# Graph layer with layernorm: the first two tiles on unsplit x in plain fp32, and the order of the first loads

## The chip, the cores and the metric

The kernel runs on one core of one Trainium2 chip. The metric is the time of one execution on the device in microseconds (us). The kernel before took 436.32 us, the median of three runs (435.46 to 437.48).

## The reference

Inputs are x (4096 x 256) and adj (4096 x 4096), both fp32. adj is nonnegative and mostly zero.

```python
def _L0_gnn_ref(cur, incidence_m):
    mask = incidence_m > 0
    head = mask.astype(incidence_m.dtype)
    head = head / jnp.maximum(jnp.sqrt(jnp.sum(head * head, axis=-1, keepdims=True)), EPS)
    inc = incidence_m + head
    edge_fea = inc @ cur
    edge_degree = jnp.sum(inc, axis=-1, keepdims=True)
    return edge_fea / edge_degree
x = _layernorm(x + _L0_gnn_ref(x, adj), axis=-1)
```

So each row of adj gets 1/sqrt(count of its positive entries) added at those entries, is multiplied with x, divided by its sum, added to x's row, and normalised.

## The kernel before, in words

**Tiling.** The output has 32 tiles of 128 rows. A tile of adj is held as `raw[:, s, k, :]`: a slot s (two, by the tile's parity) and four quarters k of 32 rows each. On the partitions a quarter is spread by columns: partition group g (32 partitions) holds columns 1024 g to 1024 g + 1023. A quarter is loaded by four DMAs of 128 KB, one for each g, in the order 0, 2, 1, 3 (L151 to L152). A 32 x 32 block transpose of the quarters gives `incT`, and its 32 blocks b are the weights of 32 steps of accumulation over the 4096 columns.

**A tile's steps.** ScalarE takes the sign of each quarter and sums it by partition (L209). TensorE sums over partition groups with `quad_sum` (`sum_signs` L533 at the start, `sum_quadrants` L545 later; the latter also sums the rows of `inc`). VectorE makes the count (L400), GpSimd takes the power 0.5 (L311), called norm. ScalarE multiplies the quarter by the norm into PSUM (L218, two buffers `scaled`). VectorE forms `inc` in units of the norm, (raw > 0) + scaled, with its row sum (L412), and transposes it (L422). The norm's factor falls out in the division by the sum.

**Products.** Of the 32 blocks six are multiplied in plain fp32 with `x_native` (L558, two instructions each, in the array `edge[s]`, columns 0 to 255). The other 26 (SPLIT) go as three products of rounded values (fp32r): incT is split in `inc_hi` (rounded, ScalarE L225 for quarters 0 and 3, GpSimd L335 for 1 and 2) and `inc_lo` (the rest, GpSimd L330), and x in high and low parts in `x_split`. One product of `inc_hi` with both parts of x (L584, 512 columns) and one of `inc_lo` with x's high part (L587, 256 columns) make one block. VectorE then adds up the residual: degree (L435), reciprocal (L439), two steps that read `edge` (L445, L449), statistics, and after GpSimd's power -0.5 (L315) the result (L470).

**Start.** SP's queue issues the four quarters of tile 0, then x's blocks 0 to 15 into slot 1 of incT, the six native blocks, tile 1, x's blocks 16 to 25 into `rows`, tile 2, and behind a wait for x's low part the residual rows. x's split is done in three chunks by ScalarE (L255), GpSimd (L341, L343, L369) and VectorE (L385). Tile 0's count and norm are taken of all four quarters at once. Tiles 0 and 1 then go as all others do, except that VectorE makes tile 0's low quarters 2 and 3 (L394).

**What sets the order.** The order of each engine's work is written out by hand; engines are tied by semaphores alone. On TensorE the sums of tile t stand behind the fourth native block of tile t, and wait for the signs of tile t + 2 (L540). VectorE's count of tile t + 1 stands behind its third `inc` quarter of tile t. GpSimd's norm of tile t + 1 is the first thing in its tile t. From tile 2 the engines run loops over pairs of tiles.

## Time and profile before

| | us |
|---|---|
| Median of three runs | 436.32 |
| The profiled execution | 437.03 |
| Its span, first to last instruction | 435.2 |
| TensorE busy | 392.1 |
| VectorE busy | 368.6 |
| GpSimd busy | 369.4 |
| ScalarE busy | 347.8 |

The mean granted clock of TensorE was 0.98 of full speed. In the profile PE is TensorE's matmul, DVE VectorE, ACT ScalarE, POOL GpSimd, SP SyncE; SPq is SP's queue of DMA issues. Busy time is a sum over the span; where it isn't spread evenly the timeline has to be read beside it. A row of a timeline has start, duration, engine, line, what is written and read, and in brackets how long the engine was idle before it and what released it.

### The profile page before, as it was taken

Reading aid. Unit: us, or ns where it says so; the run is one execution under the profiler, and the core shown is the slowest. Engines: PE = TensorE matmul, PEld = TensorE weight load, DVE = VectorE, ACT = ScalarE, POOL = GpSimd, SP = SyncE. Lnnn points to the kernel's source line nnn. Section 1 sums busy time; section 2 is a strip of 40 time slices with the busy share of each in tenths; the row PEclk is TensorE's granted clock in tenths of the full one; section 3 lists DMA queues with packets and bytes.
Section 4 is the critical chain, followed back from the end, with each engine's and each line's share of the span. In section 5 each row is a group of like instructions: output and inputs, shape, how many; then the busy total and the mean of one; then the engine's idle time right before and its main releaser. Section 6 shows DMA issues by size and latency. Waiting matters only on the chain.

```text
span 435.2 us, 8833 instructions
## 1 busy us (share of the span) xinstructions
PE 392.1 (90%) x2148; PEld 343.6 (79%) x2148; DVE 368.6 (85%) x739; ACT 347.8 (80%) x452; POOL 369.4 (85%) x274
## 2 busy tenths in 40 slices
PE   0056479999999999999999999999999999999995
PEld 0036368888888888888888888888888888888884
DVE  0436788999999999999999999999999999999932
ACT  4655899889888998988998888898889988886200
POOL 1096878999999999999999999999999999999860
PEclk9996789999999999999999999999999999999999
DMA  7999575566667766666666666666666666670010
GB/s 198 218 265 256 172 221 184 174 197 191 191 208 207 217 195 196 192 193 194 195 194 193 199 202 217 206 185 207 189 194 193 192 195 196 199 213 24 24 39 12
DMA packets 38090, 79.84 MB, mean 183 GB/s; under 512 B 9408, under 2 KB 21696, under 8 KB 38080
## 3 DMA queue, kind: packets, MB, share of 16 engines
q1 hardware_dynamic: 38080, 79.73, 63.0%
q14 instruction: 7, 0.06, 0.1%
q8 instruction: 3, 0.05, 0.0%
HBM read 75.50 MB, written 4.19 MB: 183 GB/s over the span
## 4 chain that ended last, share of the span: by engine, by line
PE 84%; SPq 5%; issue 5%; DMA 3%; DVE 2%; ACT 0%; POOLq 0%; POOL 0%; ACTq 0%; DVEq 0%
PE edge L584 42%; PE edge L587 22%; PE edge L558 19%; DMA rows<-in_x_dram 3%; SPq L152 3%; SPq L171 1%; PE sums L545 1%; DVE inc L412 1%; DVE incT L422 1%; SPq L168 1%; SPq L175 0%; ACT scaled L218 0%; POOLq L46 0%; POOL rstd L315 0%; DVE rows L449 0%
## 5 line engine op out<-in xcount | busy, mean ns | idle before, releaser
L584 PE MATMUL edge<-x_split,inc_hi 128*128 128x512 f32 (+1 forms) x864 | 304.4, 399 | 4.1 <-POOL x_split L369 2.7
L330 POOL TENSOR_TENSOR inc_lo<-incT,inc_hi 128x832 fp32r<-128x832 f32 x126 | 248.7, 1985 | 12.1 <-DVE incT L422 7.7
L587 PE MATMUL edge<-x_split,inc_lo 128*128 128x256 f32 x832 | 235.8, 283 | 0.0
L584 PEld LDWEIGHTS edge<-x_split,inc_hi 128*128 128x128 f32 x864 | 165.0, 191 | 40.6 <-POOL x_split L369 3.0
L209 ACT ACTIVATE sign_out<-raw,sign_bias 128x1024 bf16<-128x1024 f32 x128 | 146.4, 1144 | 35.4 <-DMA raw<-in_adj_dram 33.9
L412 DVE SCALAR_TENSOR_TENSOR inc<-raw,scaled 128x1024 f32<-128x1024 f32 x128 | 153.6, 1202 | 9.3 <-ACT scaled L218 9.3
L587 PEld LDWEIGHTS edge<-x_split,inc_lo 128*128 128x128 f32 x832 | 160.1, 192 | 0.0
L422 DVE STREAM_TRANSPOSE incT<-inc 128x1024 f32<-128x1024 f32 x128 | 155.4, 1227 | 0.0
L218 ACT ACTIVATE scaled<-raw,norm 128x1024 f32<-128x1024 f32 x128 | 141.6, 1108 | 9.7 <-DVE inc L412 5.3
L558 PE MATMUL edge<-x_native,incT 128*128 128x256 f32 x384 | 97.5, 394 | 11.9 <-DMA x_native<-in_x_dram 11.9
L558 PEld LDWEIGHTS edge<-x_native,incT 128*128 128x128 f32 x384 | 69.9, 194 | 20.7 <-DVE incT L422 12.0
L225 ACT CAST inc_hi<-incT 128x832 fp32r<-128x832 f32 x64 | 56.5, 884 | 13.0 <-DVE incT L422 9.0
L311 POOL TENSOR_TENSOR norm<-count,half 128x4 f32<-128x4 f32 x32 | 34.6, 1080 | 28.5 <-DVE count L400 28.5
L335 POOL TENSOR_SCALAR inc_hi<-incT 128x832 fp32r<-128x832 f32 x64 | 58.7, 918 | 0.0
L445 DVE SCALAR_TENSOR_TENSOR rows<-edge,rdeg,rows 128x256 f32<-128x256 f32 x32 | 15.5, 483 | 31.4 <-PE edge L587 31.4
L315 POOL TENSOR_TENSOR rstd<-var_eps,minus_half 128x1 f32<-128x1 f32 x32 | 18.0, 562 | 11.8 <-DVE var_eps L461 11.8
L209 ACT ACTIVATION_READ_ACCUMULATOR sign_out<-raw,sign_bias 128x1 f32 x128 | 23.9, 187 | 0.0
L470 DVE TENSOR_SCALAR rows<-rows,mean_var,rstd 128x256 f32<-128x256 f32 x32 | 20.9, 654 | 1.3 <-POOL rstd L315 1.3
L545 PEld LDWEIGHTS sums<-part_sums,quad_sum 128*128 128x128 f32 x64 | 12.2, 194 | 7.5 <-DVE incT L422 3.3
L400 DVE TENSOR_SCALAR count<-sums 128x4 f32<-128x4 f32 x32 | 4.9, 153 | 15.3 <-PE sums L533 14.0
L533 PE MATMUL sums<-part_sums,quad_sum 128*128 128x4 f32 x4 | 0.9, 307 | 16.6 <-ACT sign_out L209 16.6
L449 DVE SCALAR_TENSOR_TENSOR rows<-edge,rdeg,rows 128x256 f32<-128x256 f32 x32 | 15.4, 480 | 0.1
(30 smaller groups left out, 86.6 us busy)
## 6 DMA issues: line engine op xcount, KB each, us to landing
raw<-in_adj_dram SPq DMA_DIRECT2D x512, 128.0 KB, 2.6
rows<-in_x_dram SPq DMA_DIRECT2D x32, 128.0 KB, 2.1
out_dram<-rows SPq DMA_DIRECT2D x32, 128.0 KB, 1.8
incT<-in_x_dram SPq DMA_DIRECT2D x4, 512.0 KB, 9.9
rows<-in_x_dram SPq DMA_DIRECT2D x4, 320.0 KB, 12.3
x_native<-in_x_dram SPq DMA_DIRECT2D x4, 192.0 KB, 10.8
```

The costliest lines, as they stand in the source:

```text
L209: nc.scalar.activation(sign_out[:, :], raw[:, s, q, :], ACT.Sign, scale=SIGN_SCALE, bias=sign_bias[:, 0:1], accum_out=part_sums[:, s, 1, q ...
L218: nc.scalar.mul(scaled[q % 2][:, :], raw[:, s, q, :], norm[:, s, q:q + 1]).then_inc(scaled_ready, 1)
L225: nc.scalar.copy(hi_of(s, q), incT[:, s, 0:SPLIT, q, :]).then_inc(hi_by_act, 1)
L311: nc.gpsimd.tensor_tensor(norm[:, s, :], count[:, s, :], half[:, :], ALU.pow).then_inc(norm_ready, 1)
L330: nc.gpsimd.tensor_tensor(inc_lo[:, s, :, q, :], incT[:, s, 0:SPLIT, q, :], hi_of(s, q).bitcast(fp32), ALU.subtract).then_inc(lo_by_pool, ...
L335: nc.gpsimd.tensor_scalar(hi_of(s, q), incT[:, s, 0:SPLIT, q, :], 1.0, 1.0, ALU.mult, ALU.mult).then_inc(hi_by_pool, 1)
L412: nc.vector.scalar_tensor_tensor(inc[:, q, :], raw[:, s, q, :], 0.0, scaled[q % 2][:, :], ALU.is_gt, ALU.add, accum_out=part_sums[:, s, 0, ...
L422: nc.vector.transpose(incT[:, s, :, q, :], inc[:, q, :].rearrange("p (b j) -> p b j", j=SQ)).then_inc(incT_ready, 1)
L470: nc.vector.tensor_scalar(result[:, s, :], y[:, s, :], mean_var[:, s, 0:1], rstd[:, s:s + 1], ALU.subtract, ALU.mult).then_inc(result_read ...
L558: last = nc.tensor.matmul(edge[s][:, 0:D], incT[:, s, SPLIT + n, :, :].rearrange("p q j -> p (q j)"), x_native[:, n, :], start=(n == 0), s ...
L584: nc.tensor.matmul(edge[s][:, c0:c1], inc_hi[:, s, b, :, :].rearrange("p q j -> p (q j)"), x_split[:, b, :, :].rearrange("p h d -> p (h d) ...
L587: last = nc.tensor.matmul(edge[s][:, D:2 * D], inc_lo[:, s, b, :, :].rearrange("p q j -> p (q j)"), x_split[:, b, 0, :], start=False, stop ...
```

## The change

Tiles 0 and 1 multiply all 32 blocks in plain fp32 with unsplit x (`native_tile`). x's 26 other blocks land in a buffer `x_stage` of their own (it shares its place with the second slot of the split adjacency, which is first written for tile 3) in four chunks of 7, 7, 6 and 6 blocks, and TensorE takes them chunk by chunk. x is split later, behind the scales of tile 1: high parts by ScalarE, low parts by GpSimd (chunks 0, 1) and VectorE (2, 3). Tile 0's count and norm are made quarter by quarter. Tile 0's loads are issued half by SP and half by ScalarE. SP's order is tile 0, native x, tile 1, the chunks of x (partition groups in the order 0, 2, 1, 3), the residual rows of tiles 0 and 1, tiles 2 and 3. Rounding of adjacency begins with tile 2, and the sums of tiles 0 and 1 are placed at blocks 12 and 26 of tile 1. The residual of tiles 0 and 1 has one step in place of two, as there are no second columns of `edge`. The loops of ScalarE, GpSimd and TensorE begin at tile 4; tiles 2 and 3 are written out. The rest of the diff (counters moved by one, names) follows from this.

```diff
--- before.py
+++ after.py
...
         x_split = sb("x_split", [P, SPLIT, 2, D], fp32r)
         x_native = sb("x_native", [P, NATIVE, D], fp32)
-
-        rows = sb("rows", [P, max(7, SPLIT - B // 2), D], fp32)
+        inc_split0 = sb("inc_split0", [P, 2, SPLIT, G, SQ], fp32r)
+
+        with nc.sbuf_tensor("x_stage", [P, SPLIT, D], fp32) as x_stage:
+            pass
+        inc_split1 = sb("inc_split1", [P, 2, SPLIT, G, SQ], fp32r)
+        inc_split = [inc_split0, inc_split1]
+
+        rows = sb("rows", [P, 7, D], fp32)
...
+        X_AT = [0, 7, 14, 20, SPLIT]
+        X_LO_POOL = [0, 1]
+        X_LO_DVE = [2, 3]
 
...
 
+        def x_staged(c):
+            return x_stage[:, X_AT[c]:X_AT[c + 1], :]
+
         def hi_of(s, q):
-            return inc_hi[:, s, :, q, :]
+            return inc_split[s][:, 0, :, q, :]
+
...
-
             for k in range(G):
-                load_quarter(0, 0, k, False)
-            for g in range(G):
-                sp.dma_start(incT[SQ * g:SQ * (g + 1), 1, :, :, :].rearrange("p b q j -> p (b q j)"),
-                             x_v[g, :, 0:X_AT[2], :]).then_inc(x_in[0], 16)
-            for g in range(G):
+                for g in (0, 1):
+                    load_piece(sp, 0, 0, k, g)
+            for g in PORT_ORDER:
                 sp.dma_start(x_native[SQ * g:SQ * (g + 1), :, :], x_v[g, :, SPLIT:B, :]).then_inc(x_native_in, 16)
             for k in range(G):
                 load_quarter(1, 1, k, False)
-            for g in range(G):
-                sp.dma_start(rows[SQ * g:SQ * (g + 1), 0:SPLIT - X_AT[2], :],
-                             x_v[g, :, X_AT[2]:SPLIT, :]).then_inc(x_in[1], 16)
+            for c in range(4):
+                for g in PORT_ORDER:
+                    sp.dma_start(x_stage[SQ * g:SQ * (g + 1), X_AT[c]:X_AT[c + 1], :],
+                                 x_v[g, :, X_AT[c]:X_AT[c + 1], :]).then_inc(x_in[c], 16)
+            for s in range(2):
+                load_residual(s, s, False)
             for s in range(2):
                 for k in range(G):
                     load_quarter(2 + s, s, k, True)
-
-                sp.wait_ge(x_lo_by_pool, 2)
-                load_residual(s, s, False)
...
+            for k in range(G):
+                for g in (2, 3):
+                    load_piece(act, 0, 0, k, g)
+            act.wait_ge(consts_ready, 1)
+
+            nc.scalar.activation(table_load[:, :], sign_bias[:, :], ACT.Sign)
+
+            sign_quarter(0, 0, 0, 0, first=True, reuse=False)
+            sign_quarter(0, 0, 0, 1, reuse=False)
+            scale_quarter(0, 0, 0, first=True)
+            sign_quarter(0, 0, 0, 2, reuse=False)
+            scale_quarter(0, 0, 1, first=True)
+            sign_quarter(0, 0, 0, 3, reuse=False)
+            scale_quarter(0, 0, 2, first=True)
+            scale_quarter(0, 0, 3, first=True)
             for q in range(G):
-                sign_quarter(0, 0, 0, q, first=(q == 0), reuse=False)
-
-            def split_x_hi(c):
-
-                act.wait_ge(x_in[c // 2], X_CHUNK)
...
-            scale_quarter(0, 0, 0, False)
-            scale_quarter(0, 0, 1, False)
-            scale_quarter(0, 0, 2, False)
-            scale_quarter(0, 0, 3, False)
-            round_quarter(0, 0, 0, False)
-            split_x_hi(1)
-            for q in range(3):
                 sign_quarter(1, 1, 0, q, reuse=False)
-            round_quarter(0, 0, 3, False)
-            sign_quarter(1, 1, 0, 3, reuse=False)
-            split_x_hi(2)
-
-            scale_quarter(1, 1, 0, True)
-            scale_quarter(1, 1, 1, True)
-            sign_quarter(2, 0, 1, 0)
-            scale_quarter(1, 1, 2, True)
-            scale_quarter(1, 1, 3, True)
-            sign_quarter(2, 0, 1, 1)
-            round_quarter(1, 1, 0, False)
-            sign_quarter(2, 0, 1, 2)
-            sign_quarter(2, 0, 1, 3)
-            round_quarter(1, 1, 3, False)
-            scale_quarter(2, 0, 0, True)
-            scale_quarter(2, 0, 1, True)
+            for q in range(G):
+                scale_quarter(1, 1, q)
+            for c in range(4):
+                split_x_hi(c)
+
+            for q in range(G):
+                sign_quarter(2, 0, 1, q, reuse=False)
+            scale_quarter(2, 0, 0)
+            scale_quarter(2, 0, 1)
             sign_quarter(3, 1, 1, 0)
             sign_quarter(3, 1, 1, 1)
...
+            tile(2, 0, 1, reuse=False)
+            tile(3, 1, 1, staged=True)
+            with act.Fori(2, PAIRS - 1) as u:
...
+            for q in range(G):
+                pool.wait_ge(first_count, q + 1)
+                nc.gpsimd.tensor_tensor(norm[:, 0, q:q + 1], count[:, 0, q:q + 1], half[:, 0:1],
+                                        ALU.pow).then_inc(first_norm, 1)
             norm_of(1, 1)
-
-            pool.wait_ge(x_hi_by_act, 2)
-            nc.gpsimd.tensor_tensor(x_part(2, 1), x_stage(2), x_part(2, 0).bitcast(fp32),
-                                    ALU.subtract).then_inc(x_lo_by_pool, 1)
-            tile(1, 1, reuse=False)
-            with pool.Fori(1, PAIRS - 1) as u:
+            for c in X_LO_POOL:
+                split_x_lo(c)
+            norm_of(2, 0)
+            tile(2, 0, reuse=False)
+            tile(3, 1, staged=True)
+            with pool.Fori(2, PAIRS - 1) as u:
...
-                yield
-                after(3)
-                nc.vector.scalar_tensor_tensor(y[:, s, :], edge[s][:, 0:D], rdeg[:, :], y_main[:, :],
-                                               ALU.mult, ALU.add).then_inc(y_ready, 1)
+                if native:
+                    nc.vector.scalar_tensor_tensor(y[:, s, :], edge[s][:, 0:D], rdeg[:, :], xres[:, s, :],
...
+            first_count_of(0)
+            first_count_of(1)
+            inc_quarter(0, 0, 0, False, False)
+            first_count_of(2)
+            transpose_quarter(0, 0, 0, False, False)
+            inc_quarter(0, 0, 1, False, False)
+            first_count_of(3)
+            transpose_quarter(0, 0, 1, False, False)
+            inc_quarter(0, 0, 2, False, False)
+            transpose_quarter(0, 0, 2, False, False)
+            inc_quarter(0, 0, 3, False, False)
+            transpose_quarter(0, 0, 3, False, False)
+            count_of(1, 1)
+            for q in range(G):
+                inc_quarter(1, 1, q, True, False)
+                transpose_quarter(1, 1, q, False, False)
+            for c in X_LO_DVE:
+                split_x_lo(c)
+            count_of(2, 0)
+            tile(2, 0, 1, native=True, slot_split=False, norm_before=False)
+            tile(3, 1, 1, native=True, slot_split=False, reuse_result=False)
...
+            def native_tile(t, s, middle):
 
                 pe.wait_ge(incT_ready, G * t + G)
-                if reuse:
-
-                    pe.wait_ge(y_ready, t - 1)
+                if t == 0:
+                    pe.wait_ge(x_native_in, FOUR_DMAS)
+                for n in range(NATIVE):
+                    if n in middle:
+                        middle[n]()
+                    native_matmul(s, SPLIT + n, x_native[:, n, :], n == 0, False)
+                for b in range(SPLIT):
+                    if t == 0 and b in X_AT:
+                        pe.wait_ge(x_in[X_AT.index(b)], FOUR_DMAS)
+                    if NATIVE + b in middle:
+                        middle[NATIVE + b]()
+                    last = native_matmul(s, b, x_stage[:, b, :], False, b == SPLIT - 1)
+                return last
...
+            def split_products(t, s, first):
+
+                pe.wait_ge(lo_by_pool, G * (t - FIRST_SPLIT) + G)
...
+
+                    pe.wait_ge(x_lo_by_pool, len(X_LO_POOL))
+                    pe.wait_ge(x_lo_by_dve, len(X_LO_DVE))
...
+            for q in range(G):
+                sum_first(q)
+            native_tile(0, 0, {3: lambda: sum_signs(1, 1)}).then_inc(edge_ready, 1)
+            native_tile(1, 1, {12: lambda: sum_quadrants(0, 0, reuse=False, first=True),
+                               26: lambda: sum_quadrants(1, 1, reuse=False)}).then_inc(edge_ready, 1)
+            tile(2, 0, first=True)
+            tile(3, 1)
+            with pe.Fori(2, PAIRS - 1) as u:
```

## Rows read from the trace of the kernel before

**Rows 1.** Page, part 1: busy time of TensorE.

```profile
PE 392.1 (90%) x2148; PEld 343.6 (79%) x2148; DVE 368.6 (85%) x739; ACT 347.8 (80%) x452; POOL 369.4 (85%) x274
```

**Rows 2.** Waits of TensorE: line, releaser, us in total, times, longest.

```profile
PE edge L558 <- DMA x_native<-in_x_dram: 11.9, 1, 11.9
...
PE edge L584 <- POOL x_split L369: 2.7, 1, 2.7
```

**Rows 3.** Timeline of TensorE: start, us, line, idle before it.

```profile
25.95 5.46 PE L558 MATMUL edge<-x_native,incT 128*128 128x256 f32 x12 [11.94 <-DMA x_native<-in_x_dram]
...
37.11 0.63 PE L584 MATMUL edge<-x_split,inc_hi 128*128 128x512 f32 x1
...
37.75 0.63 PE L584 MATMUL edge<-x_split,inc_hi 128*128 128x512 f32 x1
...
51.33 0.56 PE L545 MATMUL sums<-part_sums,quad_sum 128*128 128x8 f32 x2 [3.00 <-DVE incT L422]
...
61.43 0.36 PE L545 MATMUL sums<-part_sums,quad_sum 128*128 128x8 f32 x2 [2.30 <-issue]
...
72.32 1.89 PE L558 MATMUL edge<-x_native,incT 128*128 128x256 f32 x8
74.05 0.28 PE L545 MATMUL sums<-part_sums,quad_sum 128*128 128x8 f32 x2
...
74.95 0.59 PE L584 MATMUL edge<-x_split,inc_hi 128*128 128x256 f32 x2
...
429.70 0.28 PE L587 MATMUL edge<-x_split,inc_lo 128*128 128x256 f32 x1
```

**Rows 4.** Busy by window: PE, PEld, DVE, ACT, POOL, granted clock, DMA share, GB/s.

```profile
62.50:65.80 3.30, 3.30 (x12) 2.82 (x12) 3.30 (x8) 3.30 (x5) 3.08 (x3) 0.50 0.47 140
96.20:418.20 322.00, 322.00 (x1811) 283.85 (x1811) 301.70 (x616) 277.01 (x361) 301.00 (x217) 1.00 0.61 185
```

**Rows 5.** Timeline of ScalarE: first steps that waited for a load.

```profile
4.88 1.15 ACT L209 ACTIVATE sign_out<-raw,sign_bias 128x1024 bf16<-128x1024 f32 x1 [1.12 <-DMA raw<-in_adj_dram]
...
12.06 1.15 ACT L209 ACTIVATE sign_out<-raw,sign_bias 128x1024 bf16<-128x1024 f32 x1 [1.13 <-DMA raw<-in_adj_dram]
...
27.66 1.15 ACT L209 ACTIVATE sign_out<-raw,sign_bias 128x1024 bf16<-128x1024 f32 x1 [3.43 <-DMA raw<-in_adj_dram]
...
39.22 2.32 ACT L255 CAST x_split<-rows 128x2560 fp32r<-128x2560 f32 x1 [4.75 <-DMA rows<-in_x_dram]
...
53.23 2.16 ACT L218 ACTIVATE scaled<-raw,norm 128x1024 f32<-128x1024 f32 x2 [0.43 <-POOL norm L311]
```

**Rows 6.** The same windows view, three stretches of the first loads.

```profile
14.00:16.00 2.00, 0.01 (x1) 0.00 (x0) 0.16 (x1) 0.64 (x1) 1.04 (x1) 1.00 1.12 216
26.00:28.00 2.00, 2.00 (x5) 1.65 (x6) 0.00 (x0) 0.34 (x1) 2.00 (x1) 1.00 1.06 289
44.00:46.00 2.00, 0.69 (x4) 0.33 (x3) 2.00 (x3) 2.00 (x4) 2.00 (x1) 1.00 0.30 88
```

**Rows 7.** Timeline of SyncE: the issue of tile 0's loads.

```profile
0.73 7.36 SPq L152 DMA_DIRECT2D raw<-in_adj_dram  x16
```

**Rows 8.** Timeline of VectorE: first and last of tile 0's eight operations.

```profile
16.51 1.22 DVE L412 SCALAR_TENSOR_TENSOR inc<-raw,scaled 128x1024 f32<-128x1024 f32 x1 [2.31 <-ACT scaled L218]
...
23.36 2.37 DVE L422 STREAM_TRANSPOSE incT<-inc 128x1024 f32<-128x1024 f32 x2
```

**Rows 9.** Timeline of GpSimd: norm of tile 2, then its first and last low quarters.

```profile
52.18 1.02 POOL L311 TENSOR_TENSOR norm<-count,half 128x4 f32<-128x4 f32 x1 [0.47 <-DVE count L400]
...
63.30 1.98 POOL L330 TENSOR_TENSOR inc_lo<-incT,inc_hi 128x832 fp32r<-128x832 f32 x1 [0.22 <-DVE incT L422]
...
69.63 3.93 POOL L330 TENSOR_TENSOR inc_lo<-incT,inc_hi 128x832 fp32r<-128x832 f32 x2
```

**Rows 10.** Page, part 5: line, operation, count, busy, mean ns of one.

```profile
L225 ACT CAST inc_hi<-incT 128x832 fp32r<-128x832 f32 x64 | 56.5, 884 | 13.0 <-DVE incT L422 9.0
...
L209 ACT ACTIVATION_READ_ACCUMULATOR sign_out<-raw,sign_bias 128x1 f32 x128 | 23.9, 187 | 0.0
```

More of the change, by code:

```diff
@@ L430, in after @@
                 def after(k):
[L432 to L434 removed]
+                    dve.wait_ge(dve_step, steps_to(t) + k - (1 if native and k > 2 else 0))
+                dve.wait_ge(summed, t + 2)
                 step(nc.vector.scalar_tensor_tensor(deg_pick[:, :], sums[s][:, 0:G], 1.0, own_quarter[:, :],
```

269 lines of the change are left out of this document (122 added, 147 removed).

## The prediction

> **What bounds the kernel now.** I read the page first: TensorE is busy 90% of a 435.2 us span [rows 1]. An average doesn't say where the other tenth is, so next came the list of waits of TensorE. All its larger waits lie in the first 62 us: 11.9 us for the native part of x and 2.7 us for the low part of x's third chunk [rows 2]; the timeline adds 3.0 us for the transposes of tile 1 and 2.3 us ahead of that tile's sums, and shows the rest: tile 0 starts at 25.95, tile 2 at 72.32, and the last product starts at 429.70, about 430.0 with its tail [rows 3]. So the 30 tiles 2 to 31 take 357.7 us, 11.92 each, and no wait stands among them. From 72.32 on TensorE sets the pace; before that the start does. The change can gain only what it takes off the start of tile 2, and what it adds before that costs nothing as long as tile 2 is ready earlier.
>
> Two prices come out of the same rows. Four native blocks go from 72.32 to 74.05, 0.433 us each. A whole tile less its six natives (2.60) and its sums (0.14) leaves 9.18 us for 26 split blocks, 0.353 each. Those are at the full clock (2.4 GHz). At the half clock the twelve native instructions from 25.95 take 5.46 us, 0.88 to 0.91 a block [rows 3], and one split block 0.64 us (37.11 to 37.75) [rows 3]. The granted clock was 0.50 in 62.5 to 65.8 too, right behind the gap that ended at 61.43 [rows 3, 4]: a gap of two to three microseconds in TensorE's work is followed by some 3 us at half clock. For those 3.3 us TensorE does work worth 1.8 us.
>
> **The terms.** (1) *Plain products for tiles 0 and 1.* Each has 32 blocks of 0.433, 13.9 us, in place of 11.8: 2.1 us more per tile, 4.2 in all at full clock. In exchange tile 0 needs no rounding, no low parts and no split x. Those were what spread tile 0 of before over 25.95 to about 56.4. TensorE is the cover of nothing here; it is fed by the loads.
>
> (2) *Order of loads.* Before, ScalarE's signs show the landings: tile 0's quarters at 4.9 to 12.06, the first quarter of tile 1 at 27.66, the last chunk of x at 39.22 [rows 5]; tile 2's data were in about 44.6 (the last window moves 0.18 MB, 0.6 us at full rate) [rows 6]. Rows of x (1 KB each) came at 216 GB/s, adjacency at 289 [rows 6]. Now tile 1 comes ahead of the 2.10 MB of x that stood before it: 9.7 us at 216 GB/s earlier, so its last quarter lands about 23 and not 33, and its signs end about 24.2. The last chunk of x has the same bytes ahead of it as before. Tile 2 has 0.26 MB more ahead, the two residual tiles, which SP now issues first and without their wait for x's low part: 1.2 us.
>
> (3) *Two queues for tile 0.* SP issued 16 loads in 7.36 us, 0.46 each [rows 7]; the halving of the first four saves 0.9 us at the front. The first four quarters land 2.4 us apart (7.2 us for three) [rows 5], more than the 1.84 that SP needs to issue four, so behind the first quarter it is the transfers that count. I take 0.5 us for all the stream, bounds 0 and 1.1. The eight issues sit on ScalarE ahead of the table load, and can move its first sign from 4.88 to about 6; tile 0's norm by quarters gains more than that (its scale no longer waits for the fourth sign), and TensorE has slack there, next. The Trainium skill (DMA: Bandwidth & Descriptors, section Issuing engines are not separate DMA queues) says that issuing from several engines saves only the time of issuing. By that rule the term would be 0.9 us at most; by a doubled rate of the first 2.1 MB it would be over 4.
>
> (4) *Tile 0.* VectorE's eight operations take 9.2 us in a chain (16.51 to 25.73 before) [rows 8]. Started some 6 us sooner they end about 19 to 20.5. TensorE then does three native blocks and waits in the middle of tile 0 for the signs of tile 1 (24.2). So the start of tile 0 is hidden, and neither the norm by quarters nor the second queue can move the end: their worth in the sum is nil. If tile 1's loads weren't there the cover would be gone, and VectorE's 20 would count.
>
> (5) *TensorE up to the sums of tile 0.* These now stand at block 12 of tile 1. From 24.4 it has 29 blocks of tile 0 and 12 of tile 1. With 5.3 us at half clock (6 blocks) and 35 at 0.433, 20.5 us: 44.9, if x is never late. By the last chunk of x (39.2 less 0.5, then 6 + 12 blocks, 7.8 us) it is 46.5. The same sums wait for tile 2's four signs: data at 44.6 + 1.2 − 0.5 = 45.3, the last sign 1.15 us: 46.4. Three roads meet at about 46.5, which I take (bounds 44.9 and 49).
>
> (6) *From there a new chain.* Sums to norm 0.85 and 1.05 for the norm (51.33, 52.18, 53.23): scale of tile 2 starts at 48.4 [rows 3, 5, 9]. ScalarE then has two scales (2.16), two signs, a scale, two signs; a sign takes 1.15 and 0.19 for its accumulator read when another sign follows, a scale 1.1 [rows 5, 10]. That is 8.3 us: 56.7. The sums of tile 1 (block 26) wait for exactly these four signs of tile 3; TensorE is there at 46.5 + 0.3 + 14 x 0.433 = 52.9, a **new wait of 3.8 us**. Queued behind that wait are the last six blocks of tile 1. VectorE waits for the same sums in its count of tile 3, with the transposes of quarters 1 to 3 of tile 2 behind it, and GpSimd waits for that count in its norm of tile 3, with all rounding of tile 2 behind it. Norm 57.6 to 58.6; then GpSimd's low and rounded quarters of tile 2, which took 63.30 to 73.56 before (last row 69.63 + 3.93), 10.3 us [rows 9]: **ready at 69.0 and not 73.56**. TensorE's natives of tile 2 start at about 62.8 (transposes) and hold the sums that wait for tile 4's signs: one round of ScalarE (four signs, four scales of 1.1, two roundings of 0.88: 10.9 us) behind 56.7, 67.6; then sums and two native blocks at half clock: **split blocks from 69.8, not 74.95** [rows 3]. Gain 5.1.
>
> (7) *The clock.* TensorE idles before 56.7, before 62.8 and before 67.6, so by the rows of (1) the split blocks start at half clock. I take 1.8 us lost (bounds 0 and 2.4).
>
> (8) *Behind tile 2.* TensorE ends tile 2 at 69.8 + 9.2 + 1.8 = 80.8 against 84.24 before. Then it needs tile 3's low parts at 83.5: GpSimd's next round of 11.3 us ends at 80.3. In the steady part GpSimd is busy 301 of 322 us [rows 4], 11.1 of each 11.92, so it can follow a TensorE that is ahead but can't catch up if it is late itself. Nothing else in the loops changes.
>
> **Sum.** 84.24 − 80.8 = 3.4 us earlier. The profiled execution took 437.03, 1.83 more than its span and 0.71 over the median 436.32. 437.03 − 3.4 = 433.6; against the median 432.9. That is the forecast: of a start that looks 15 us better for tile 0, some 3 arrive. Its own range is 431 to 435.
>
> **Rivals.**
> *A, slower: the half clock in tile 1's plain products.* x's chunks (0.92 MB each, 4.2 us at 216 GB/s) come slower than TensorE eats them at full clock (7 x 0.433 = 3.0 us), so it idles over 1 us per chunk. For: the natives at 25.95 stayed at half speed for all of their 5.4 us, and short idle stretches were followed by clock 0.50 [rows 3, 4]. Against: at half clock seven blocks take 6.2 us, longer than a chunk, so TensorE has no gap then and warms again. If the last 6 and the first 12 blocks run at half clock, the sums of tile 0 come 18 x 0.45 = 8 us later, and all of (6) with them: 432.9 + 8 = 440.9. It decides from 3.4 us of loss on, eight cold blocks.
>
> *B, faster: x lands sooner and the clock holds.* Before, x was loaded in the order of partitions 0, 32, 64, 96, 512 KB at a time, at 216 GB/s; the adjacency, in the order 0, 64, 32, 96, at 289 [rows 6]. The change gives x that second order as well. If it is the order and not the packet's size that makes the rate, x's 4.19 MB come 4.9 us sooner, TensorE is never starved in tile 0, and (5) gives 44.9, 1.6 us more; with a warm clock in (7) another 1.8: 432.9 − 3.4 = 429.5. The Trainium skill (SBUF — State Buffer, section Door 1: The DMA port swizzle) has partitions 32 apart on the same ports and 64 apart on others; by that rule this rival's first half happens. The start of the stream, in the better order and at 0.52 MB per 2.4 us, 219 GB/s [rows 5], speaks against counting on all of it.
>
> *C, no change: the new chain is longer than I have it.* It has some 20 links from tile 2's last sign to tile 2's low part, on four engines. GpSimd was busy 301 of 322 us in the steady part [rows 4], so nothing lost there comes back. Three microseconds more (late landings of tiles 2 and 3, tile 2's products cold throughout) give 436. That the first tiles gain nothing at all, because the last x chunk lands as late as before, is the same case.
>
> **How the numbers follow.** Forecast 0.45, A 0.13, B 0.22, C 0.20. Measurement can tell about 0.5% (2.2 us) of this kernel from no change, so faster is below 434.1: the forecast but for its upper end, and B: 0.62. Same: C and the upper end of the forecast, 0.25. Slower: A, 0.13. The range takes B with its bounds and leaves out most of A: 428.5 to 438.
>
> **What would show it.** The step on loads: ScalarE's first sign of tile 1 near 17 to 18, last chunk of x near 38.7 (B: near 34). Step 5: sums of tile 0 near 46.5 (A: over 52). Step 6: a wait of 3 to 4 us of TensorE for a sign of tile 3, GpSimd's last low part of tile 2 ending near 69. Step 7: granted clock 0.50 somewhere in 57 to 73. Step 8: tile 3 starting near 80.8, tiles of 11.92 behind it with no wait. If a wait appears in those, or if the sums of tile 0 come after 50, the prediction is wrong.

## The result and the profile after

The changed kernel takes 432.73 us against 436.83 (medians of 20 runs each): ratio 0.9903, 95% interval [0.9889, 0.9917], 4.1 us faster. Its profiled execution took 431.71, 1.0 under its median, where the one of before lay within 0.7 of its own; so the 5.3 us between the two spans (435.2 and 429.9) are more than the change brings as a rule.

TensorE, start, duration, line, idle before it; these rows answer to [rows 3]:

```profile
20.55 2.93 PE L577 MATMUL edge<-x_native,incT 128*128 128x256 f32 x6 [6.43 <-DVE incT L436]
...
29.24 6.15 PE L577 MATMUL edge<-x_stage,incT 128*128 128x256 f32 x26 [0.54 <-DMA x_stage<-in_x_dram]
36.15 2.86 PE L577 MATMUL edge<-x_stage,incT 128*128 128x256 f32 x12 [0.76 <-DMA x_stage<-in_x_dram]
38.84 2.75 PE L577 MATMUL edge<-x_native,incT 128*128 128x256 f32 x12
...
46.34 0.36 PE L572 MATMUL sums<-part_sums,quad_sum 128*128 128x8 f32 x2 [2.16 <-issue]
...
56.29 0.36 PE L572 MATMUL sums<-part_sums,quad_sum 128*128 128x8 f32 x2 [1.75 <-issue]
...
61.71 1.99 PE L577 MATMUL edge<-x_native,incT 128*128 128x256 f32 x8 [0.85 <-DVE incT L436]
66.75 0.36 PE L572 MATMUL sums<-part_sums,quad_sum 128*128 128x8 f32 x2 [3.04 <-DVE incT L436]
...
68.23 0.79 PE L618 MATMUL edge<-x_split,inc_split 128*128 128x256 f32 x2
...
78.75 1.89 PE L577 MATMUL edge<-x_native,incT 128*128 128x256 f32 x8
```

Tile 0 is done at 38.84, where before it was at about 56.4. Tile 3 starts at 78.75 against 84.24: of 17.6 us at the end of tile 0 a third is left two tiles later. The rows between show where it goes: TensorE stands at the sums of tile 0 (46.34), at those of tile 1 (56.29), for the transposes of tile 2 (61.71) and at the sums of tile 2 (66.75). The profile puts the first of them down to "issue" and the last to VectorE's transposes; the first names no engine and the last one whose work had long been done; the semaphore that came last was that of ScalarE's signs, as the next rows show.

ScalarE; these rows answer to [rows 5]:

```profile
17.78 1.15 ACT L220 ACTIVATE sign_out<-raw,sign_bias 128x1024 bf16<-128x1024 f32 x1 [0.36 <-DMA raw<-in_adj_dram]
...
36.12 1.48 ACT L247 CAST x_split<-x_stage 128x1536 fp32r<-128x1536 f32 x1 [0.55 <-DMA x_stage<-in_x_dram]
39.09 1.15 ACT L220 ACTIVATE sign_out<-raw,sign_bias 128x1024 bf16<-128x1024 f32 x1 [1.49 <-DMA raw<-in_adj_dram]
...
45.01 1.15 ACT L220 ACTIVATE sign_out<-raw,sign_bias 128x1024 bf16<-128x1024 f32 x1 [0.96 <-DMA raw<-in_adj_dram]
...
54.95 1.15 ACT L220 ACTIVATE sign_out<-raw,sign_bias 128x1024 bf16<-128x1024 f32 x1
...
65.41 1.15 ACT L220 ACTIVATE sign_out<-raw,sign_bias 128x1024 bf16<-128x1024 f32 x1
```

The last sign of tile 2 waits for its load until 45.01 and ends at 46.16; the sums of tile 0 start at 46.34. The last sign of tile 3 (54.95) ends at 56.10, the sums of tile 1 start at 56.29; the last of tile 4 ends at 66.56, the sums of tile 2 start at 66.75. Three times TensorE starts 0.2 us behind a sign.

GpSimd; these rows answer to [rows 9]:

```profile
56.93 1.01 POOL L324 TENSOR_TENSOR norm<-count,half 128x4 f32<-128x4 f32 x1 [8.93 <-DVE count L408]
58.08 1.96 POOL L344 TENSOR_TENSOR inc_split<-incT,inc_split 128x832 fp32r<-128x832 f32 x1
...
64.32 3.86 POOL L344 TENSOR_TENSOR inc_split<-incT,inc_split 128x832 fp32r<-128x832 f32 x2
```

GpSimd idles 8.93 us for the count of tile 3, then needs 10.1 us and has the low parts of tile 2 at 68.18; TensorE's split blocks start at 68.23. By window (busy time of PE, PEld, DVE, ACT, POOL, then granted clock, DMA share, GB/s; compare [rows 4, 6]):

```profile
2.00:12.00 10.00, 1.73 (x6) 1.50 (x6) 1.57 (x5) 6.73 (x10) 2.18 (x9) 1.00 1.04 278
28.00:34.00 6.00, 5.46 (x25) 4.17 (x24) 5.93 (x8) 4.72 (x4) 1.30 (x1) 1.00 1.13 240
46.00:56.00 10.00, 8.19 (x30) 6.60 (x30) 5.77 (x13) 8.03 (x12) 1.01 (x1) 0.83 0.81 226
58.00:62.00 4.00, 3.15 (x8) 1.98 (x8) 4.00 (x8) 4.00 (x6) 3.92 (x4) 0.62 0.37 107
66.00:71.00 5.00, 4.15 (x16) 3.38 (x17) 5.00 (x12) 4.59 (x7) 4.99 (x4) 0.69 0.81 250
96.20:418.20 322.00, 322.00 (x1812) 283.01 (x1811) 299.28 (x614) 271.74 (x354) 298.54 (x215) 1.00 0.59 181
```

The first 10 us of loads run at 278 GB/s and x in 28 to 34 at 240, against 216 for x before [rows 6]; the clock falls three times behind TensorE's waits (0.83, 0.62, 0.69 as means of these windows), and the steady part is what it was: TensorE busy 322.00 of 322 us.

### The profile page after: what moved, and what is told of

Read it like the earlier page. It is cut to its first block, busy times and chain, and to the rows that moved or that the text cites. A ratio compares the mean times of both kernels' runs of the same rounds, so it can differ in the third digit from the quotient of the medians.

```text
span 429.9 us, 8836 instructions
## 1 busy us (share of the span) xinstructions
PE 396.9 (92%) x2152; PEld 344.8 (80%) x2152; DVE 371.7 (86%) x739; ACT 346.5 (81%) x450; POOL 351.1 (82%) x266
## 3 DMA queue, kind: packets, MB, share of 16 engines
q10 hardware_dynamic: 384, 1.05, 0.8%
## 4 chain that ended last, share of the span: by engine, by line
PE 84%; SPq 5%; issue 4%; POOL 2%; DMA 2%; DVE 1%; POOLq 0%
PE edge L618 41%; PE edge L577 21%; PE edge L621 21%; SPq L187 3%; SPq L157 2%; DMA x_stage<-in_x_dram 2%; POOL inc_split L344 2%; PE sums L572 1%; SPq L182 0%; POOL inc_split L349 0%; DVE incT L436 0%; POOL rstd L328 0%; POOLq L45 0%; DVE rows L463 0%; DVE rows L467 0%
## 5 line engine op out<-in xcount | busy, mean ns | idle before, releaser
L618 PE MATMUL edge<-x_split,inc_split 128*128 128x512 f32 (+1 forms) x810 | 281.4, 396 | 0.1
L344 POOL TENSOR_TENSOR inc_split<-incT,inc_split 128x832 fp32r<-128x832 f32 x120 | 237.2, 1987 | 10.5 <-DVE incT L436 7.6
L621 PE MATMUL edge<-x_split,inc_split 128*128 128x256 f32 x780 | 218.3, 280 | 0.0
L618 PEld LDWEIGHTS edge<-x_split,inc_split 128*128 128x128 f32 x810 | 152.9, 189 | 34.9 <-POOL inc_split L344 0.6
L220 ACT ACTIVATE sign_out<-raw,sign_bias 128x1024 bf16<-128x1024 f32 x128 | 146.4, 1144 | 32.4 <-DMA raw<-in_adj_dram 30.9
L621 PEld LDWEIGHTS edge<-x_split,inc_split 128*128 128x128 f32 x780 | 147.7, 189 | 0.0
L242 ACT CAST inc_split<-incT 128x832 fp32r<-128x832 f32 x60 | 53.2, 886 | 11.8 <-DVE incT L436 7.3
L349 POOL TENSOR_SCALAR inc_split<-incT 128x832 fp32r<-128x832 f32 x60 | 55.2, 920 | 0.0
L463 DVE SCALAR_TENSOR_TENSOR rows<-edge,rdeg,rows 128x256 f32<-128x256 f32 x30 | 14.5, 484 | 31.0 <-PE edge L621 31.0
L577 PE MATMUL edge<-x_stage,incT 128*128 128x256 f32 x104 | 27.4, 422 | 1.6 <-DMA x_stage<-in_x_dram 1.6
L577 PEld LDWEIGHTS edge<-x_stage,incT 128*128 128x128 f32 x104 | 21.3, 209 | 6.5 <-DMA x_stage<-in_x_dram 3.2
L488 DVE TENSOR_SCALAR rows<-rows,mean_var,rstd 128x256 f32<-128x256 f32 x32 | 21.8, 681 | 1.3 <-POOL rstd L328 1.3
L355 POOL TENSOR_TENSOR x_split<-x_stage,x_split 128x1792 fp32r<-128x1792 f32 x2 | 9.5, 4772 | 7.7 <-ACT x_split L247 7.7
```

Of the source, the lines that this page charges most:

```text
L220: nc.scalar.activation(sign_out[:, :], raw[:, s, q, :], ACT.Sign, scale=SIGN_SCALE, bias=sign_bias[:, 0:1], accum_out=part_sums[:, s, 1, q ...
L242: nc.scalar.copy(hi_of(s, q), incT[:, s, 0:SPLIT, q, :]).then_inc(hi_by_act, 1)
L344: nc.gpsimd.tensor_tensor(lo_of(s, q), incT[:, s, 0:SPLIT, q, :], hi_of(s, q).bitcast(fp32), ALU.subtract).then_inc(lo_by_pool, 1)
L349: nc.gpsimd.tensor_scalar(hi_of(s, q), incT[:, s, 0:SPLIT, q, :], 1.0, 1.0, ALU.mult, ALU.mult).then_inc(hi_by_pool, 1)
L488: nc.vector.tensor_scalar(result[:, s, :], y[:, s, :], mean_var[:, s, 0:1], rstd[:, s:s + 1], ALU.subtract, ALU.mult).then_inc(result_read ...
L577: return nc.tensor.matmul(edge[s][:, 0:D], incT[:, s, b, :, :].rearrange("p q j -> p (q j)"), x_of_b, start=start, stop=stop)
```

## The experiments

The times are medians, those of the kernel before beside them 436.25 to 436.83; "changed" is the changed kernel. From the timelines of each profile come the marks: the start of the last sign of tile 2 on ScalarE, of the sums of tiles 0 and 1 and of tile 3 on TensorE, and the end of the low parts of tile 2 on GpSimd. The chain is low parts less sums of tile 0; the last column but one is from there to tile 3's start.

| kernel | last sign of tile 2 | sums, tile 0 | sums, tile 1 | low parts, tile 2 | tile 3 | chain | then | us |
|---|---|---|---|---|---|---|---|---|
| changed | 45.01 | 46.34 | 56.29 | 68.18 | 78.75 | 21.8 | 10.6 | 432.73 |
| after_again | 45.96 | 47.30 | 57.24 | 69.35 | 78.69 | 22.1 | 9.3 | 433.10 |
| one_queue | 45.39 | 46.73 | 56.88 | 68.77 | 80.73 | 22.0 | 12.0 | 433.23 |
| x_order | 48.83 | 50.17 | 60.32 | 72.22 | 83.90 | 22.1 | 11.7 | 433.63 |
| norm_at_once | 43.46 | 44.80 | 55.16 | 67.26 | 78.01 | 22.5 | 10.8 | 431.14 |
| resid_late | 44.94 | 46.28 | 56.22 | 68.13 | 78.51 | 21.9 | 10.4 | 431.15 |
| more_plain | 41.74 | 45.98 | 55.85 | 67.95 | 77.13 | 22.0 | 9.2 | 432.69 |
| more_plain20 | 46.34 | 53.15 | 63.01 | 74.91 | 85.66 | 21.8 | 10.8 | 438.04 |
| reorder | 46.59 | 47.93 | 59.26 | 68.26 | 83.14 | 20.3 | 14.9 | 436.05 |
| best1 | 43.15 | 44.49 | 56.20 | 65.49 | 80.46 | 21.0 | 15.0 | 436.35 |
| reorder2 | 47.37 | 48.71 | 60.14 | 69.28 | 78.83 | 20.6 | 9.6 | 432.26 |
| best2 | 44.04 | 45.38 | 57.03 | 66.17 | 75.59 | 20.8 | 9.4 | 430.91 |
| best3 | 43.14 | 44.48 | 55.91 | 65.26 | 74.85 | 20.8 | 9.6 | 430.82 |

One difference ties the marks to the times. The time of the profiled execution less the start of tile 3 is 352.8 us in the kernel before (437.03 less 84.24) and 352.7 to 353.0 in the changed kernel and the seven below it, down to more_plain20: there the start of tile 3 carries the whole difference. In reorder and best1 it is 353.8 and 353.3, in reorder2, best2 and best3 354.8, 355.0 and 356.1: these three lose 2 to 3 us again behind the start of tile 3.

**The changed kernel once more** (no edit).

> The changed kernel as it is, beside the others of this set. Its profiles so far: from the sums of tile 0 to tile 2's last low part 21.8 to 22.5 us in five kernels, and from there to tile 3's start 10.4 to 12.0. Theory (a rigid chain): the same here, 21.8 to 22.5. Rival (the chain breathes with the loads): over 23 or under 21.

433.10 us, ratio 0.9912 [0.9884, 0.994]. The chain is 22.1, as expected. Over the eight kernels that leave it alone it is 21.8 to 22.5 while its start moves between 44.8 and 53.15: step 6's road is rigid. What follows it is not (9.2 to 12.0), though it is the same 26 blocks.

**One queue for tile 0.**

```diff
             for k in range(G):
-                for g in (0, 1):
-                    load_piece(sp, 0, 0, k, g)
+                load_quarter(0, 0, k, False)
...
-            for k in range(G):
-                for g in (2, 3):
-                    load_piece(act, 0, 0, k, g)
```

> The changed kernel with all 16 loads of tile 0 issued by SyncE and none by ScalarE. My theory now: the start is tied to the stream of loads (tile 2's last sign waits for a load at 45.01 in the changed kernel), and two queues moved 0.40 MB more by 12 us than one queue did before, 1.4 us of stream. So everything from the x chunks on lands 0.9 to 1.4 us later, the sums of tile 0 go from 46.3 to about 47.4, and the kernel takes 1.1 us more. Rival 1: two queues save only the time of issuing: at most 0.9 us. Rival 2: the front of the stream is hidden: 0.

433.23, ratio 0.9923 [0.9897, 0.995]. By window (columns as above), its loads ran at 250 GB/s in 2 to 12 us:

```profile
2.00:12.00 10.00, 1.73 (x6) 1.50 (x6) 1.95 (x6) 6.02 (x11) 2.35 (x10) 1.00 0.91 250
```

With two queues it was 278, and 265 to 283 in all twelve profiles with two queues: 0.28 MB, 1.2 us at 240 GB/s. That is more than the 0.9 us of issuing that I had put down for the first quarter, but issuing isn't ruled out as the cause. One queue issues 128 KB per 0.46 us [rows 7], 285 GB/s at most, over all of tile 0, and the DMA share was 0.91 where it was 0.99 to 1.05 with two; no run separates the pace of issuing from the rate of transfer. In time little can be seen: x's last chunk started to be rounded at 36.30 (changed: 36.12), tile 2's last sign at 45.39 (45.01), both less than the profiles differ among themselves, and the 0.5 us by the medians lies inside both intervals. The rate is shown; that it brings anything in time is not.

**Order of x's pieces.**

```diff
-            for g in PORT_ORDER:
+            for g in range(G):
                 sp.dma_start(x_native[...], ...)
...
-                for g in PORT_ORDER:
+                for g in range(G):
                     sp.dma_start(x_stage[...], ...)
```

> The changed kernel with the loads of x (chunks and native blocks) in the order of partition groups 0, 1, 2, 3 in place of 0, 2, 1, 3. If the order makes the rate, x's 4.19 MB fall back from 240 GB/s to the 216 of the kernel before: 1.9 us more of stream, last chunk of x landing near 38 and not 36.1, sums of tile 0 near 48.2, kernel 1.9 us slower. If the rate is that of 1 KB rows whatever their order: no change in rate (240) and time.

433.63, ratio 0.9937 [0.9912, 0.9962]: 0.9 us slower than the changed kernel by the medians, 1.5 by the ratios, with intervals that just overlap. Its profiled execution took 436.74, 3.1 over its median, so its marks (last chunk at 38.41, sums of tile 0 at 50.17) show the direction, not the size. Busy time, clock, DMA share and GB/s by window:

```profile
28.00:34.00 6.00, 6.00 (x27) 4.96 (x25) 5.89 (x9) 4.46 (x4) 0.55 (x1) 1.00 1.14 220
```

220 against 240 GB/s with nothing but the order different; the twelve profiles in the other order have 230 to 263 in this window, so 220 lies below them all. So both expectations are half right: the order makes about a tenth of the rate of x, and most of the distance to the 289 GB/s of the adjacency [rows 6] is left. That this rest is due to the 1 KB rows is likely, but no run changes their size alone. The Trainium skill's rule on ports (SBUF — State Buffer, Door 1: The DMA port swizzle) agrees in direction.

**Tile 0's norm at once.**

```diff
             sign_quarter(0, 0, 0, 1, reuse=False)
-            scale_quarter(0, 0, 0, first=True)
             sign_quarter(0, 0, 0, 2, reuse=False)
-            scale_quarter(0, 0, 1, first=True)
             sign_quarter(0, 0, 0, 3, reuse=False)
+            scale_quarter(0, 0, 0, first=True)
+            scale_quarter(0, 0, 1, first=True)
```

> The changed kernel with ScalarE's four signs of tile 0 ahead of its scales, so that the norm by quarters brings nothing. My theory (term 4): VectorE ends tile 0 some 2.3 us later (22.8, not 20.5), TensorE has 2.2 us of slack ahead of the sums of tile 0, so the time changes by 0 to 0.3 us. Rival: TensorE's start sets the end: 2.3 us slower.

431.14, ratio 0.9884 [0.9858, 0.9909]. By the timeline TensorE starts tile 0 at 22.44 and not 20.55, and doesn't wait for x behind it:

```profile
22.44 2.93 PE L577 MATMUL edge<-x_native,incT 128*128 128x256 f32 x6 [10.16 <-DVE incT L436]
25.16 0.43 PE L557 MATMUL sums<-part_sums,quad_sum 128*128 128x4 f32 x2
25.45 2.15 PE L577 MATMUL edge<-x_native,incT 128*128 128x256 f32 x6
27.43 11.39 PE L577 MATMUL edge<-x_stage,incT 128*128 128x256 f32 x52
38.66 2.75 PE L577 MATMUL edge<-x_native,incT 128*128 128x256 f32 x12
```

Tile 0 ends at 38.66, where the changed kernel ends it at 38.84: two microseconds of start are gone without a trace. The norm by quarters brings nothing here. That the kernel is 1.6 us faster by the medians, 0.8 by the ratios, isn't explained; the intervals overlap, and its profile had tile 2's last quarter 1.5 us sooner than the changed kernel's, which this edit doesn't touch.

**Residual rows behind tile 2.**

```diff
-            for s in range(2):
-                load_residual(s, s, False)
             for s in range(2):
                 for k in range(G):
                     load_quarter(2 + s, s, k, True)
+                if s == 0:
+                    for r in range(2):
+                        load_residual(r, r, False)
```

> The changed kernel with the two residual loads (0.26 MB) issued behind tile 2's loads in place of ahead of them. My theory: tile 2's last quarter gates the chain signs, sums of tile 0, norm, scales; it lands 1.1 us earlier, the sums of tile 0 go from 46.3 to 45.2 and the kernel gains 1.1 us. Rival: TensorE's own work or x's last chunk gates: no change.

431.15, ratio 0.9874 [0.9841, 0.9907]: 1.6 us under the changed kernel by the medians, with overlapping intervals. Its own profile doesn't show the gain (last sign of tile 2 at 44.94); the profiles of reorder and best1, and of reorder2 and best2, which differ by this edit alone, have it 3.4 and 3.3 us earlier. One profile each is thin: over all kernels whose loads aren't changed the mark lies between 41.74 and 47.37. In time reorder to best1 is nothing and reorder2 to best2 1.35 us.

**Ten and twenty more plain products.** They stand ahead of block 6 of tile 1 and write columns that nobody reads, so the output is unchanged.

```diff
+                    if t == 1 and b == 0:
+                        for n in range(10):
+                            nc.tensor.matmul(edge[s][:, D:2 * D], incT[:, s, n, :, :]...,
+                                             x_stage[:, n, :], start=False, stop=False)
```

> The changed kernel with ten more plain products (10 x 0.433 = 4.3 us at full clock) in tile 1, ahead of the sums of tile 0; they write columns of the array that nothing reads. My theory: TensorE has 0.8 to 2.2 us of slack there, so that the price of the plain products shows only beyond it: sums of tile 0 near 48.5 to 49, kernel 2.1 to 3.5 us slower. If TensorE's work in tiles 0 and 1 were not near the path at all: 0. If it were all on it: 4.3.

432.69, ratio 0.9903 [0.9879, 0.9928]: the ten cost nothing that can be measured (the intervals leave room for 1 us); I had expected 2.1 to 3.5. In its own profile they weren't free. Tile 2's last sign ended at 42.89, the earliest of all, and TensorE came to the sums only at 45.98, without a gap: there TensorE's road was the last, by 2.9 us. How much is covered depends on when tile 2 lands.

> As more_plain (products that write columns nobody reads, ahead of the sums of tile 0), with twenty in place of ten: 8.7 us. Ten cost nothing that the times show; their profile had the sums of tile 0 at 45.98 behind an uninterrupted TensorE, where the last sign of tile 2 had ended 3 us before. My theory: cover of 2 to 3 us, then full price. TensorE reaches the sums of tile 0 at about 50 to 53, the chain of 21.8 to 22.5 us follows, and the kernel is 4 to 6.5 us slower than the changed one (437 to 439). Rival: TensorE's work in tiles 0 and 1 has wide cover, since ten cost nothing: under 1.5 us.

438.04, ratio 1.0027 [1.0008, 1.0045]: twenty cost 5.3 us against the changed kernel. If every block beyond the cover costs its full 0.433 us, the cover is 3.4 us (8.7 less 5.3); by medians alone this is good to about 1 us. TensorE of that kernel:

```profile
43.65 7.07 PE L594 MATMUL edge<-x_stage,incT 128*128 128x256 f32 x32
50.56 2.75 PE L577 MATMUL edge<-x_stage,incT 128*128 128x256 f32 x12
53.15 0.28 PE L572 MATMUL sums<-part_sums,quad_sum 128*128 128x8 f32 x2
```

TensorE runs into the sums without a gap at 53.15, though the last sign of tile 2 had ended at 47.49, and 32.5 us later tile 3 starts (32.4 in the changed kernel). So what the change adds ahead of these sums (2.9 of its 4.2 us, 44 of the 64 blocks) lies under the loads, and some 3.4 us more would; behind that each block costs its 0.43 us. The other 1.3 us stand behind the sums, where TensorE waits for ScalarE anyway (1.75 us at the sums of tile 1, 3.04 at those of tile 2).

**The chain loosened.** The same instructions in tiles 2 and 3, in other places: ScalarE rounds quarters 0 and 3 of tile 2 and quarter 0 of tile 3 earlier, VectorE transposes quarter 1 ahead of the count, GpSimd does its first two steps ahead of the norm, TensorE's sums of tiles 1 and 2 stand later.

```diff
 # ScalarE
             sign_quarter(4, 0, 2, 0)
+            round_quarter(2, 0, 3, False)
             scale_quarter(3, 1, 0)
             sign_quarter(4, 0, 2, 1)
...
             scale_quarter(3, 1, 2)
+            round_quarter(3, 1, 0, True, True)
             sign_quarter(4, 0, 2, 2)
             sign_quarter(4, 0, 2, 3)
...
 # GpSimd, tile 2 and 3
-                norm_of(t + 1, 1 - s)
-                low_quarter(t, s, 0, reuse, behind=1)
+                low_quarter(t, s, 0, reuse, behind=0)
+                pool.wait_ge(incT_ready, G * t + 2)
                 round_quarter(t, s, 1)
+                norm_of(t + 1, 1 - s)
...
 # TensorE
-            native_tile(1, 1, {12: ..., 26: lambda: sum_quadrants(1, 1, reuse=False)})
+            native_tile(1, 1, {12: ..., 30: lambda: sum_quadrants(1, 1, reuse=False)})
```

> The changed kernel with the new chain of step 6 loosened in tiles 2 and 3 only: ScalarE rounds quarter 0 ahead of the signs and takes the first sign of tile 3 in the wait for the norm, VectorE transposes quarter 1 ahead of the count, GpSimd makes the low part of quarter 0 and rounds quarter 1 ahead of the norm, TensorE has the sums of tile 1 at block 30 and those of tile 2 behind its sixth split block. The same instructions, other places. My theory (the chain through sums of tile 1, count, norm and GpSimd's round sets tile 2's end): tile 2's low parts ready at 65 and not 68.2, and 2 us of this kept (GpSimd's low parts of tile 3 come next): 1.5 to 3 us faster than the changed kernel. Rival (loads and ScalarE's signs of tile 4 or the clock set it): within 0.5 us.

436.05, ratio 0.9965 [0.9947, 0.9983]: 3.3 us slower than the changed kernel, where I expected 1.5 to 3 faster. The low parts of tile 2 came 20.3 us behind the sums of tile 0 and not 21.8; I had expected some 18.7 (65 less 46.3), so half of the gain in the chain was there. The loss came behind it, as the next profile shows: I had put two of ScalarE's roundings ahead of signs of tile 4.

> The kernel reorder with the residual loads issued behind tile 2's loads as well. Theory: 1.1 us more than reorder, as the sums of tile 0 still hang on tile 2's last load: 2.6 to 4 us faster than the changed kernel. Rival: the loads' landing varies by as much from run to run, and it takes what reorder takes.

436.35, ratio 0.999 [0.9969, 1.0011]. I had expected 2.6 to 4 us less than the changed kernel; it takes 3.6 more. The timeline of ScalarE in best1:

```profile
60.60 0.89 ACT L243 CAST inc_split<-incT 128x832 fp32r<-128x832 f32 x1 [2.33 <-DVE incT L471]
68.11 0.89 ACT L243 CAST inc_split<-incT 128x832 fp32r<-128x832 f32 x1 [2.40 <-DVE incT L471]
```

and of TensorE:

```profile
71.58 0.36 PE L628 MATMUL sums<-part_sums,quad_sum 128*128 128x8 f32 x2 [3.51 <-DVE incT L471]
```

The low parts were ready at 65.49, the split blocks began at 65.55, and then TensorE stood 3.5 us at the sums of tile 2. These wait for tile 4's signs, and the signs stood on ScalarE behind the two roundings, which waited 4.7 us for transposes.

**ScalarE's order mended.** ScalarE keeps the changed kernel's order, but that a scale and the rounding of quarter 0 of tile 2 stand ahead of three signs of tile 3; the sums of tile 2 stand behind its third split block, not its sixth. best2 has the residual rows late as well.

```diff
             sign_quarter(3, 1, 1, 0)
-            sign_quarter(3, 1, 1, 1)
             scale_quarter(2, 0, 2)
+            round_quarter(2, 0, 0, False)
+            sign_quarter(3, 1, 1, 1)
             sign_quarter(3, 1, 1, 2)
             sign_quarter(3, 1, 1, 3)
-            round_quarter(2, 0, 0, False)
             scale_quarter(2, 0, 3)
```

> The kernel reorder with ScalarE's order mended. Its profile showed low parts of tile 2 early, but ScalarE stood 2.3 and 2.4 us in two roundings that wait for transposes, with the signs of tile 4 behind them, and TensorE stood 3.5 us at the sums of tile 2 for those signs. Here ScalarE keeps the changed kernel's order but for the rounding of tile 2's quarter 0, which goes ahead of three signs of tile 3; the sums of tile 2 stand behind its third split block. Theory: low parts of tile 2 ready 21 us and not 21.8 to 22.5 behind the sums of tile 0 or sooner (19.5 to 20.5), no wait of TensorE above 1 us behind them, 1.5 to 2 us faster than the changed kernel (431). Rival: the gain is taken by another in-order wait again: 433 or more.

432.26, ratio 0.9884 [0.9856, 0.9911]: 3.8 us better than reorder, and level with the changed kernel, where I had expected 1.5 to 2 us less. The chain is 20.6, and from the low parts to tile 3 it is 9.6 us and not 14.9.

> reorder2 with the residual loads behind tile 2's loads. Theory: 1 to 1.5 us more than reorder2: 429.5 to 430.5. Rival (loads' landing is noise): as reorder2.

430.91, ratio 0.9869 [0.9843, 0.9896]: 1.8 us under the changed kernel by the medians, its interval just touching the other's, but only 0.2 under resid_late, which has the same loads and the chain left alone. Tile 3 starts at 75.59, 2.9 us sooner than there. TensorE's next wait, at the sums of tile 3:

```profile
79.40 0.36 PE L618 MATMUL sums<-part_sums,quad_sum 128*128 128x8 f32 x2 [1.92 <-issue]
```

**The next wait taken away too** (VectorE and GpSimd of tile 3 in the changed kernel's order, the sums of tile 3 behind its third split block).

> best2 with the changed kernel's order of VectorE and GpSimd for tile 3 (only tile 2 has the loosened one), and the sums of tile 3 behind its third split block as well. In best2's profile tile 3 started at 75.6 and not 78.7, but its sums then stood 2 us for the last sign of tile 5, and tile 3's low parts came 12.8 us behind tile 2's and not 11.2. Theory (each in-order wait of the start hands over to the next): tile 3's low parts near 77.5, tile 4 starting 1 to 2 us earlier than best2's 89.6, 429 to 430. Rival (the lead can't be kept, the next tile's wait takes it): 430.5 or more.

430.82, ratio 0.9883 [0.9855, 0.991]. Tile 3 starts at 74.85, and GpSimd gives the lead back. Its timeline:

```profile
67.79 1.02 POOL L334 TENSOR_TENSOR norm<-count,half 128x4 f32<-128x4 f32 x1 [2.53 <-DVE count L433]
```

and TensorE's, in tile 3:

```profile
79.35 0.50 PE L666 MATMUL edge<-x_split,inc_split 128*128 128x256 f32 x2 [1.75 <-POOL inc_split L354]
```

The sums no longer stop TensorE; GpSimd's low parts of tile 3 do, because its norm of tile 4 waits for the count, and that for the sums that were moved back. Tile 4 starts at 88.84 against 89.58 in best2, where I had expected 1 to 2 us. The rival was right: this lead isn't kept past GpSimd. best2 and best3 have the lowest medians of the study, some 1.9 us under the changed kernel, with intervals that touch or overlap its own; resid_late and norm_at_once are within 0.4 us of them.

## Why the prediction was right

The forecast was 432.9, with 431 to 435 as its own range; 432.73 was measured. That the two lie 0.2 us apart is partly luck. The forecast took 3.4 us off a median of three runs, 436.32; beside the changed kernel the kernel before took 436.83, and the gain was 4.1. In the profiles tile 3 starts 5.5 us earlier, not 3.4. The direction and the road that sets the size are right, the size is a sixth low by the medians. The steps, with the marks of the profile after:

| step | foreseen | measured |
|---|---|---|
| 2, signs of tile 1 begin | 17 to 18 | 16.2, first wait for a load at 17.78 |
| 2, last chunk of x | 38.7 (B: 34) | 36.15 |
| 4, tile 0's transposes end | 19 to 20.5 | 20.5 |
| 5, sums of tile 0 | 46.5 | 46.34 |
| 6, sums of tile 1 | 56.7 | 56.29 |
| 6, wait of TensorE there | 3.8 | 1.75 |
| 6, low parts of tile 2 | 69.0 | 68.18 |
| 6, split blocks begin | 69.8 | 68.23 |
| 7, lost to the half clock | 1.8 | 1.3 (68.23 to 78.75, less 9.18) |
| 8, tile 3 starts | 80.8 | 78.75 |

**Terms 1 and 4, hidden work.** norm_at_once and more_plain show it: starting tile 0 two microseconds later, or 4.3 us more of plain products, costs nothing that can be measured. The sums of tile 0 wait for the latest of three roads, and the plain products are on one with slack. I had put that slack at nothing (three roads meeting at 46.5); it was 2.2 us in the profile after, and 3.4 by more_plain20. The reason is x: TensorE is fed sooner, as term 2 took 216 GB/s for x and it came at 240.

**Term 3.** 278 against 250 GB/s is 1.2 us. The 0.5 us that I took is also one_queue's distance by the medians, but that lies within the intervals and confirms nothing. The Trainium skill's rule (DMA: Bandwidth & Descriptors, Issuing engines are not separate DMA queues) isn't refuted by the 1.2 us: my 0.9 counted the issues of the first quarter alone, and all sixteen took 7.36 us by one queue [rows 7] and 3.74 by two.

**Term 5, the mis-sized part.** TensorE had done its 12 blocks of tile 1 at 44.2, where I had 44.9 to 46.5. Only the signs' road (tile 2's last sign) came out as foreseen, and it alone set 46.34. That too was luck in part: two errors cancel in it. The last chunk of x was there 2.5 us sooner than I had it (36.15, not 38.7), but from there to tile 2's last quarter it took 8.9 us (to 45.01) and not 6.6 (to 45.3). Had tile 2 followed at the pace that I took, the sums of tile 0 would have come at TensorE's 44.2. The mark moves by 5 us between profiles, so one profile can't confirm it to a few tenths.

**Term 6** carried the prediction. The new wait is there, as is what is queued behind it on three engines. Its size at TensorE was off by half: I had TensorE at the sums of tile 1 at 52.9, at full clock. The 14 blocks ahead of them took 7.98 us and not 6.1, as the clock had fallen behind the 2.16 us at the sums of tile 0 (0.83 in 46 to 56). That took nothing from the end: a wait costs by when it ends, and that is ScalarE's. The chain can be had a little shorter (20.3 to 21.0 in the last five kernels, 21.8 to 22.5 in the others), but hardly any of it reaches the end: reorder2 is 0.5 us under the changed kernel, best3 0.3 under resid_late, both within the intervals. The difference below the table of marks says where the rest goes: 2 to 3 us are lost behind the start of tile 3.

**Term 7.** From the low parts to tile 3's start the 26 blocks take 9.2 us at full clock. The eight kernels that leave the chain alone have 9.2 to 12.0: the half clock costs 0 to 2.8, where I had 0 to 2.4. The 1.8 us that I took from rows 3 and 4 was a slip: it is the work that TensorE did in 3.3 us at half clock, and the loss was 1.5; 1.3 was measured. TensorE's wait at the sums of tile 2 just ahead doesn't tell how much is lost: 2.59 us stands before both the 9.3 of after_again and the 12.0 of one_queue. The last section shows what differs between these two.

**The rivals.** A (half clock in tile 1) didn't happen: the blocks of tile 1 from 38.84 took 2.75 us for six, full speed, and in tile 0 TensorE never waited over 0.8 us for x. What A says of the price, that a delay at the sums of tile 0 goes straight to the end, was right, as more_plain20 shows by other means: TensorE reached the sums 6.8 us later, tile 3 started 6.9 us later, and the kernel was no longer faster than the one before. B happened in part: x at 240 and not 216, but TensorE's road wasn't the late one, so it brought little. C (a chain three microseconds longer) didn't happen: from the sums of tile 0 to the low parts of tile 2 it was 21.8 us, where the forecast had 22.5.

## What to carry over

Where a start is fed by loads, find which road comes last at the first point where roads meet; here some 6 us of work on another road were free (2.9 of the change, 3.4 more by more_plain20), and a sooner start there (tile 0's norm by quarters) brought nothing. Behind that point follow the chain through each engine's order up to the first tile of the steady part: a wait in an in-order queue costs what stands behind it, and two roundings placed 2.4 us too early on ScalarE undid more than the loosened chain had won. Judge such a start by marks (sums, low parts, first steady tile) in several profiles, since loads and clock move each run by as much as the edits do.
